# Value projections, a combination, gathers and the last block's running sums in other ticks of a hand-ordered megakernel

## The chip, the cores and the metric

One core of one Trainium2 chip runs one program. The metric is the device time of an execution in microseconds. TensorE (PE), VectorE (DVE), ScalarE (ACT), GpSimd (POOL) and the sync engine (SP, which only issues transfers) each run an instruction stream of their own and meet at semaphores.

## The reference, cut to what matters

x is 16 sequences of 256 tokens with 128 features, all fp32. Two layers, each `x = x + s * silu(g)` with s and g computed from the layer-normed x:

```
layer 0: s = causal softmax attention (16 heads of 64) @ Wo + bo
         g = shared FFN (352 wide) + the FFN of the token's best of 8 experts
layer 1: s = linear attention: phi = elu + 1, 16 heads of 8,
             num, den = running sums over the sequence of k*v and of k
         g = a network of 2 layers, each:
             h = shift_token(x); q, k, v = h @ wqkv   (8 heads of 64)
             q, k normed, rotated (xpos); attention in a window of 64 tokens
             x = x + o @ wo
             h = layer norm of shift_token(x); a, g = h @ w1 + b1
             x = x + (a * gelu(g)) @ w2 + b2
```

## The kernel before

The tokens are worked through in 8 blocks (b = 0 to 7) of 512 tokens: two sequences, four tiles of 128 tokens. All attention is done in steps of one form, whatever the layer: for a pair of heads and one sequence, TensorE computes logits, VectorE adds the mask and takes the maximum (L1041, "masked"), ScalarE takes exponentials (L871, L872, "exps"), TensorE transposes them (L595), VectorE and ScalarE copy the result out (L1052, L886), TensorE multiplies with the values (L615 or L629, "values"), and for every second step a transposition of the inverse sums (L639, "merge") is copied out by ScalarE (L849) and multiplied on (L1063).

The order is written out by hand in the class `Plan`. It makes a list of ticks; a tick holds at most one attention step, and `self.put(tick, name, ...)` lays side work into a tick. Every engine then walks through the same ticks and emits its share in a fixed order: TensorE emits the projections or transpositions of q and k for a later step ("produce"), the step's logits, the previous step's transpositions, the side work, and then the product of values two steps back and its merge. ScalarE emits its copies, then the side work, then the exponentials, then the merge's copy. VectorE emits masking, copy and scaling first and the side work last. GpSimd and SP do only side work, and GpSimd the expansion of the inverse sums (L1341). A tick is no barrier: each queue runs in order and as far ahead as its semaphores let it.

A block's softmax attention has the name (0, b, half, pair), and its first ticks are f0 (half 0) and f1 (half 1). The ticks from block 1 on repeat every 36. The side work that the change touches:

- `v` (b, half, t): value projection of tile t of a half, one product of 512 columns on TensorE (L545) and one copy on ScalarE (L849). Values are needed two ticks behind f0 or f1.
- `down0`, `comb` (b): the shared FFN's second product (L672) and, on VectorE, the addition of the expert's result (L1094); then the combination: a tanh on ScalarE (L915) and three operations on VectorE (L1100, L1102, L1104). Both stand at tick c of the block, `comb` one tick later where `late` is set (blocks 3 to 6).
- `r` (b): four indirect gathers of the expert results from DRAM, issued by GpSimd (L1377), into the buffer `c.r` that is also `c.xn0`. `held` is the planner's list of tick spans in which that buffer is in use; `down0` waits for the gathers.
- `kv`, `cum`, `sum`, `o1`, `oT`, `s1` (b): the linear attention. `kv` forms the products k*v of a tile on GpSimd (L1441, 1152 columns) and adds two tiles (L1445); `cum` is the running sum of one of eight chunks, one product on TensorE (L740), a copy on ScalarE (L900) and four operations on GpSimd (L1411 to L1416); `sum` reduces the chunk on VectorE (L1206); `o1` divides, `oT` transposes, `s1` is the output product (L751). In ticks they are laid out from l0 on.

The other side work named below: `qkv`, `mix`, `rot`, `rr`, `kn` make q and k of the windowed attention: a square and a copy on ScalarE (L950, L951), the rotary products on VectorE (L1227, L1231, L1236) and GpSimd (L1456, L1457), an inverse root by Newton steps on VectorE in twelve small instructions of 64 columns (L1241, L291 to L296), and the scaling of the keys (L1327). `ln2`, `ln2n`, `yT` are the second layer norm: moments and inverse root on VectorE, whitening (L315), transposition on TensorE (L540). `ffn` is the shared FFN's first product.

All products on TensorE are fp32 and take two passes, so one product is two records; transpositions take one.

## Time and profile before

| | us |
|---|---|
| median of 3 runs | 2084.16 (2081.3 to 2085.23) |
| the profiled execution | 2096.84 |
| its span | 2095.0 |
| mean granted clock of TensorE in it | 0.918 |
| busy: TensorE products / weight loads | 1780.8 / 1150.7 |
| busy: VectorE / ScalarE / GpSimd | 1283.2 / 1186.3 / 868.5 |

A busy figure is the time in which the engine executed something; idle time is noted at the instruction that ends it, with what released it. The granted clock is TensorE's, as a share of 2.4 GHz; it has the values 1 and 0.5, and a stretch shows the mean. Times inside the execution are counted from the start of its span. The chain of waits runs 48% on TensorE, 20% on VectorE and 7% on ScalarE. Transfers take part in the first 270 us mostly; after that the 16 DMA engines are nearly idle.

Which tick stands where in the trace was found by counting instructions in program order. Tick 80 starts on TensorE at about 578 us, tick 116 at 805, tick 152 at 1037, tick 188 at 1269, tick 224 at 1501, tick 256 at 1708, tick 286 at 1915 and tick 299 at 2013.

### The profile page before, as it was taken

To read this page: it belongs to the slowest core of one execution; us is meant where nothing else is said; L and a number is where in the kernel's file an instruction comes from. 1 tells how busy PE (TensorE), PEld (TensorE's weight loads), DVE (VectorE), ACT (ScalarE), POOL (GpSimd) and SP (SyncE) were. 2 spreads that over 40 slices of the span, in tenths; PEclk is the share of its full clock that TensorE was granted. 3 is DMA by queue.
4 is the path that set the end of the run, shared out by engine and by line. 5 is a ranking of instruction groups with operands and counts; after the bars stand their busy time and mean duration, and the time that the engine had idled before them with its cause. 6 is when DMAs were issued, how large, how long until landed. Compare 5 with 4: busy or idle time off the path is not lost.

```text
span 2095.0 us, 38065 instructions
## 1 busy us (share of the span) xinstructions
PE 1780.8 (85%) x12532; PEld 1150.7 (55%) x12532; DVE 1283.2 (61%) x4211; ACT 1186.3 (57%) x3527; POOL 868.5 (41%) x993
## 2 busy tenths in 40 slices
PE   6679988998989888998889988988889897785876
PEld 4358754654566455664565456554556455463554
DVE  4434446556675567566756566656756656868663
ACT  2444547565756575657656675657556565553643
POOL 2633215533535334432544344533553345646410
PEclk9889999999999999999999999999999998898978
DMA  8146600000000000000000000000000000000000
GB/s 230 52 157 208 193 16 1 11 1 1 6 2 16 1 1 6 6 12 1 6 1 17 1 1 6 16 1 1 6 2 11 0 6 1 1 7 0 1 1 11
DMA packets 49725, 53.48 MB, mean 26 GB/s; under 512 B 6387, under 2 KB 42237, under 8 KB 49533
## 3 DMA queue, kind: packets, MB, share of 16 engines
q0 software_dynamic: 7808, 27.79, 4.0%
q1 hardware_dynamic: 41724, 23.26, 3.9%
q8 instruction: 104, 1.70, 0.3%
q14 instruction: 89, 0.72, 0.1%
HBM read 41.60 MB, written 9.44 MB: 24 GB/s over the span
## 4 chain that ended last, share of the span: by engine, by line
PE 48%; DVE 20%; ACT 7%; issue 6%; POOL 1%; DVEq 0%; ACTq 0%; POOLq 0%
PE ps L595 5%; PE ps L657 4%; PE ps L554 3%; PE ps L732 3%; PE ps L574 3%; DVE p L1041 3%; DVE big L1231 3%; PE ps L615 3%; PE ps L629 2%; PE ps L639 2%; DVE ss L1227 2%; PE ps L564 2%; PE ps L783 2%; PE ps L774 2%; PE ps L776 2%
## 5 line engine op out<-in xcount | busy, mean ns | idle before, releaser
L1341 POOL COPY rdx<-rden 128x256 f32<-128x256 f32 x256 | 100.8, 423 | 659.0 <-DVE rden L1058 633.9
L1041 DVE CUSTOM_DVE_ANT_0 p<-ps,mask 128x128 f32<-128x128 f32 (+1 forms) x512 | 152.2, 353 | 222.7 <-PE ps L587 216.5
L1041 DVE CUSTOM_DVE_ANT_0 p<-ps,mask,nrq 128x128 f32<-128x128 f32 x512 | 148.8, 346 | 189.1 <-PE ps L583 188.3
L595 PE MATMUL ps<-ident,p 128*128 128x128 f32 x1280 | 223.8, 300 | 27.0 <-ACT p L872 25.2
L871 ACT ACTIVATE p<-p,nmax 128x128 f32<-128x128 f32 x512 | 200.2, 391 | 52.9 <-DVE nmax L1041 52.6
L872 ACT ACTIVATE p<-p,nmax 128x128 f32<-128x128 f32 (+1 forms) x512 | 226.2, 442 | 0.0
L886 ACT ACTIVATE pt<-ps 128x384 f32<-128x384 f32 (+1 forms) x256 | 111.7, 436 | 195.8 <-PE ps L595 194.3
L732 PE MATMUL ps<-wqkv,hT 128*128 128x512 f32 x384 | 197.2, 622 | 27.5 <-ACT big L951 25.8
L595 PEld LDWEIGHTS ps<-ident,p 128*128 128x128 f32 x1280 | 146.4, 149 | 106.6 <-issue 91.0
L574 PE MATMUL ps<-k,q 64*128 64x128 f32 x1024 | 132.1, 335 | 45.1 <-DVE nmax L1041 24.2
L574 PEld LDWEIGHTS ps<-k,q 64*128 64x128 f32 x1024 | 82.0, 194 | 148.6 <-issue 85.3
L1052 DVE COPY pt<-ps 128x384 f32<-128x384 f32 (+1 forms) x256 | 124.4, 486 | 59.0 <-PE ps L595 58.9
L564 PE MATMUL ps<-ident,big 128*128 128x128 f32 x512 | 86.5, 308 | 80.2 <-DVE big L1236 37.1
L1456 POOL TENSOR_TENSOR big<-big,rots 128x512 f32<-128x512 f32 x64 | 98.1, 1533 | 124.5 <-ACT big L951 124.5
L554 PE MATMUL ps<-xnT,w 128*128 128x512 f32 x256 | 148.3, 665 | 0.9 <-ACT v L849 0.9
L615 PEld LDWEIGHTS ps<-pt,v 128*64 128x64 f32 (+1 forms) x2048 | 107.2, 138 | 71.7 <-issue 49.7
L615 PE MATMUL ps<-pt,v 64*64 64x64 f32 (+2 forms) x2048 | 143.2, 258 | 0.2 <-PE ps L615 0.2
L732 PEld LDWEIGHTS ps<-wqkv,hT 128*128 128x128 f32 x384 | 62.9, 190 | 129.3 <-ACT big L951 77.9
L657 PE MATMUL ps<-wo,attT 128*128 128x128 f32 x1024 | 125.1, 282 | 7.5 <-DVE nmax L1041 5.1
L657 PEld LDWEIGHTS ps<-wo,attT 128*128 128x128 f32 x1024 | 120.9, 197 | 12.9 <-DVE nmax L1041 9.4
L849 ACT ACTIVATE rT<-ps 128x512 f32<-128x512 f32 x128 | 74.8, 584 | 82.0 <-PE ps L639 81.4
L564 PEld LDWEIGHTS ps<-ident,big 128*128 128x128 f32 x512 | 65.2, 158 | 96.8 <-issue 68.7
(255 smaller groups left out, 4151.0 us busy)
## 6 DMA issues: line engine op xcount, KB each, us to landing
slots_in<-xn SPq DMA_DIRECT2D x1, 2560.0 KB, 14.3
v<-slots_in SPq DMA_DIRECT2D x20, 128.0 KB
slots_out<-v SPq DMA_DIRECT2D x20, 128.0 KB
big<-in_x SPq DMA_DIRECT2D x4, 512.0 KB, 6.0
x<-in_x SPq DMA_DIRECT2D x8, 256.0 KB, 3.9
out_x<-x SPq DMA_DIRECT2D x8, 256.0 KB, 2.3
wqkv<-in_wqkv SPq DMA_DIRECT2D x2, 768.0 KB
xn<-in_x SPq DMA_DIRECT2D x6, 256.0 KB, 3.1
```

The costliest lines, as they stand in the source:

```text
L554: MM(bank[:, :], c.wqk[which][:, a:a + P], c.xnT[:, st.b % 2, :], start=True, stop=True).then_inc(c.mm_full, 1)
L564: last = nc.tensor.transpose(bank[:, t * P:(t + 1) * P], c.qkr[:, t, a:a + P], c.ident[:, :])
L574: MM(banks[h][:, 0:P], q[f:f + HD, 0:P], k[f:f + HD, 0:P], start=True, stop=True)
L595: last = nc.tensor.transpose(bank[:, j * P:(j + 1) * P], c.p[:, u % 4, j * P:(j + 1) * P], c.ident[:, :])
L615: last = MM(bank[f:f + HD, q + at:q + end], v[keys, 2 * st.s + t, a:a + HD], pts[h][keys, at:end], **flags)
L657: last = MM(bank[:, t * P:(t + 1) * P], c.attT[kind][:, i, t * P:(t + 1) * P], w, start=i == 0, stop=i == END)
L732: MM(bank[:, :], c.hT[:, t * P:(t + 1) * P], c.wqkv[:, l, i * INNER1:(i + 1) * INNER1], start=True, stop=True).then_inc(c.mm_full, 1)
L871: A(p[:, 0:P], p[:, 0:P], ACT.Exp, bias=c.nmax[:, u % 4, 0:1], scale=-1.0, accum_out=den[:, 0:1])
L872: A(p[:, P:end], p[:, P:end], ACT.Exp, bias=c.nmax[:, u % 4, 1:2], scale=-1.0, accum_out=den[:, 1:2])\
L886: A(c.pt[:, u % 4, 0:end], c.pt_ps[pt.slot("t", st.n, 1)][:, 0:end], ACT.Copy).then_inc(c.pt_done_act, 1)
L1041: last = V.tensor_tensor_reduce(out=c.p[:, u % 4, a:b], in0=bank[:, a:b], in1=mask, scale=scale, scalar=3e38, op0=ALU.add, op1=ALU.min, ac ...
L1052: V.tensor_copy(c.pt[:, u % 4, 0:end], bank[:, 0:end]).then_inc(c.pt_done, 1)
```

## The change

Nothing is computed otherwise and nothing is added or left out; instructions change their place in the queues. In ticks, as the planner's rules give them before and after:

| side work | blocks | before | after |
|---|---|---|---|
| `v` half 0, tile 2 | 3 to 7 | 71, 107, 143, 179, 215 | 70, 106, 142, 178, 214 |
| `v` half 1, tiles 0 and 1 | 3 to 7 | 80, 116, 152, 188, 224 | 87, 123, 159, 195, 231 |
| `v` half 1, tiles 2 and 3 | 3 to 7 | 88, 124, 160, 196, 232 | 97, 133, 169, 205, 241 |
| `r` | 3 to 6 | 114, 150, 186, 222 | 110, 146, 182, 218 |
| `comb` | 3 to 6 | 117, 153, 189, 225 | 116, 152, 188, 224 |
| `kv` tiles 0, 1 | 7 | 279, 280 | 289, 290 |
| `kv` tiles 2, 3 | 7 | 285 | 295 |
| `cum`, eight chunks | 7 | 281, 282, 285, 286, 289 to 292 | 291, 292, 295, 296, 299 to 302 |
| `sum`, eight chunks | 7 | a tick behind each | a tick behind each |
| `o1`, `oT`, `s1` | 7 | 295, 297, 298 | 305, 307, 308 |

All else keeps its tick, and the number of ticks stays 322. The span in which the buffer of the gathers counts as held grows from three ticks to seven for blocks 3 to 6.

```diff
--- before.py
+++ after.py
@@ -224,7 +224,7 @@
                 self.put(a + 3 + t, "lin", b, t)
                 self.put(a + 5 + t, "phi", b, t)
             self.qkv_stages(a + 4, b, 0)
-            l0 = self.first[(1, b, 0, 0)] + (7 if b == LAST else 0)
+            l0 = self.first[(1, b, 0, 0)] + (17 if b == LAST else 0)
             for t in range(2):
                 self.put(l0 - 1 + t, "kv", b, t)
             for n, at in enumerate((1, 2, 5, 6, 9, 10, 11, 12)):
@@ -251,26 +251,27 @@
                 assert x1 > shared[b - 2], b
             for t in range(TILES):
                 if b:
-                    self.put(f0 - (2 if b < XRING else 11 - t // 2), "v", b, 0, t)
-                self.put(f1 - 3 if b < XRING else f0 - 1 if t < 2 else f0 + 7, "v", b, 1, t)
+                    self.put(f0 - (2 if b < XRING else 11 - t // 3), "v", b, 0, t)
+                self.put(f1 - 3 if b < XRING else f0 + 6 if t < 2 else f1, "v", b, 1, t)
             late = 4 if XRING <= b < LAST else 0
             for half in range(2):
                 self.put(self.end[(0, b, half, PAIRS - 1)] + 4 + (late - 1 if late and half else 0), "wo", 0, b, half)
             c = max(self.end[(0, b, 1, PAIRS - 1)] + 4, e_end + 3) + late
-            while any(c - 3 - late <= y and x <= c + 1 for x, y in busy) or any(c - 2 <= y and x <= c for x, y in held):
+            ahead = 6 if late else 2
+            while any(c - 3 - late <= y and x <= c + 1 for x, y in busy) or any(c - ahead <= y and x <= c for x, y in held):
                 c += 1
             assert c < lead[b] - (8 if 0 < b < LAST else 0), (b, c, lead[b])
             for ch in range(3):
                 self.put(c - 3 - late + ch, "ffn", b, ch)
             if b >= XRING:
                 at = max(f1, self.end[(1, b - XRING, 1, PAIRS - 1)] + 12)
-                assert at <= c - 2, (b, at, c)
+                assert at <= c - ahead, (b, at, c)
                 self.put(at, "xres", b)
             shared[b] = c - 1
-            held.append((c - 2, c))
-            self.put(c - 2, "r", b)
+            held.append((c - ahead, c))
+            self.put(c - ahead, "r", b)
             self.put(c, "down0", b)
-            self.put(c + (late > 0), "comb", b)
+            self.put(c, "comb", b)
             busy.append((c - 3 - late, c + 1))
         self.length = max(len(self.ticks), max(self.side) + 1) + 4
```

## Rows read from the trace of the kernel before

**Rows 1.** Table of stretches: busy us (instructions) by engine, granted clock, DMA share.

```profile
821.00:1051.00 230.00, 203.61 (x1445) 127.58 (x1446) 149.86 (x498) 141.00 (x424) 98.27 (x112) 0.94 0.02 6
...
1888.00:2013.00 125.00, 83.57 (x557) 52.44 (x557) 93.74 (x194) 58.49 (x153) 64.61 (x62) 0.81 0.00 1
```

**Rows 2.** VectorE in time order (start, us, operation, idle before), ticks 116 to 120.

```profile
816.37 0.69 DVE L1094 TENSOR_TENSOR ff<-ps,xn 128x512 f32<-128x512 f32 x1 [0.97 <-PE ps L672]
...
820.97 0.29 DVE L1041 CUSTOM_DVE_ANT_0 p<-ps,mask 128x128 f32<-128x128 f32 x1 [3.91 <-PE ps L587]
...
824.00 2.60 DVE L1102 TENSOR_TENSOR ff<-ff,s_sb 128x512 f32<-128x512 f32 x1
...
836.84 0.35 DVE L1041 CUSTOM_DVE_ANT_0 p<-ps,mask,nrq 128x128 f32<-128x128 f32 x1 [2.71 <-PE ps L583]
```

**Rows 3.** VectorE in order of time, block 2's combination and the ticks behind.

```profile
560.47 0.69 DVE L1094 TENSOR_TENSOR ff<-ps,xn 128x512 f32<-128x512 f32 x1 [1.99 <-PE ps L672]
...
562.58 0.69 DVE L1102 TENSOR_TENSOR ff<-ff,s_sb 128x512 f32<-128x512 f32 x1
...
591.31 0.28 DVE L1041 CUSTOM_DVE_ANT_0 p<-ps,mask 128x128 f32<-128x128 f32 x1
...
604.75 0.35 DVE L1041 CUSTOM_DVE_ANT_0 p<-ps,mask,nrq 128x128 f32<-128x128 f32 x1 [1.14 <-PE ps L583]
```

**Rows 4.** TensorE in order of time, around ticks 116, 124 and 134.

```profile
816.17 1.02 PE L545 MATMUL ps<-w,xnT 128*128 128x512 f32 x2
...
858.35 0.63 PE L540 MATMUL ps<-ident,h 128*128 128x128 f32 x4 [2.99 <-DVE h L315]
...
859.94 3.24 PE L545 MATMUL ps<-w,xnT 128*128 128x512 f32 x4 [0.26 <-ACT xT L968]
...
918.18 1.08 PE L540 MATMUL ps<-ident,h 128*128 128x128 f32 x4 [2.82 <-DVE h L315]
```

**Rows 5.** All engines in order of time, 815 to 832 us: GpSimd's key-value product.

```profile
823.38 2.67 POOL L1441 TENSOR_TENSOR big<-qkb,v 128x1152 f32<-128x1152 f32 x1
```

**Rows 6.** VectorE in order of time, first masking of tick 125.

```profile
866.50 0.35 DVE L1041 CUSTOM_DVE_ANT_0 p<-ps,mask,nrq 128x128 f32<-128x128 f32 x1 [6.88 <-PE ps L583]
```

**Rows 7.** ScalarE in order of time, end of the exponentials of tick 123.

```profile
854.61 0.19 ACT L872 ACTIVATION_READ_ACCUMULATOR p<-p,nmax 128x1 f32 x1
```

**Rows 8.** Table of stretches, behind the layer norm's transposition of tick 134.

```profile
917.00:923.80 6.80, 5.62 (x21) 3.47 (x22) 4.19 (x19) 3.39 (x11) 0.00 (x0) 0.51 0.00 0
```

**Rows 9.** VectorE in order of time, scaling of the keys in tick 107.

```profile
748.53 2.84 DVE L1327 TENSOR_TENSOR big<-big,rr 128x512 f32<-128x512 f32 x4
```

**Rows 10.** The gathers' line (min/median/max ns), then GpSimd, then VectorE in order of time.

```profile
L1377 POOL DMA_INDIRECT xn<-slots_out,pos_i x32: 940/955/1891, 284.3 to 1702.4; - x32
...
771.45 0.74 POOL L1341 COPY rdx<-rden 128x256 f32<-128x256 f32 x2 [3.35 <-DVE rden L1058]
...
775.40 1.26 POOL L1457 TENSOR_TENSOR big<-big,rots 128x512 f32<-128x512 f32 x1
...
782.03 1.30 DVE L1236 TENSOR_TENSOR big<-big 128x1024 f32<-128x1024 f32 x1
```

**Rows 11.** Table of stretches, the small instructions of the last two rotary steps.

```profile
1921.70:1933.60 11.90, 0.54 (x3) 0.14 (x1) 11.50 (x12) 0.60 (x1) 11.09 (x9) 0.50 0.00 0
...
2001.10:2003.90 2.80, 2.75 (x14) 2.45 (x14) 2.42 (x12) 0.98 (x2) 0.00 (x0) 0.50 0.02 6
```

**Rows 12.** VectorE in order of time, ticks 286 and 287.

```profile
1925.35 2.14 DVE L295 TENSOR_TENSOR scratch<-scratch,ss 128x64 f32<-128x64 f32 x1
...
1935.05 1.23 DVE L1206 TENSOR_REDUCE v<-v 128x36 f32<-128x288 f32 x2
```

**Rows 13.** GpSimd in order of time, tick 285.

```profile
1923.02 4.38 POOL L1441 TENSOR_TENSOR w<-attT 128x1152 f32<-128x1152 f32 x2
...
1927.48 2.61 POOL L1445 TENSOR_TENSOR w<-w 128x1152 f32<-128x1152 f32 x1
```

**Rows 14.** TensorE in order of time, tick 298.

```profile
2009.58 1.92 PE L751 MATMUL ps<-lwo,xT 128*128 128x128 f32 x8
```

## Prediction, before the changed kernel was run

> **What bounds the kernel now.** I read the table of stretches first, then the chain of waits, then the order of time around each place that the change touches. In one period of 36 ticks (one block's softmax attention and one block's second branch, 230 us) TensorE is busy for 203.6 us, VectorE for 149.9, ScalarE for 141 [rows 1]. So TensorE sets the time, and what can be won in a period is its idle time and the stretches in which it runs at 1.2 instead of 2.4 GHz. In the last stage VectorE has 93.7 of 125 us and the granted clock is 0.81 [rows 1]: there VectorE's own chain (rotary products, norms, running sums) sets the time.  The dates below are those of block 3's combination and block 4's value projections, which repeat every 231 us.
>
> **Part 1: the combination of blocks 3 to 6 one tick earlier, two value projections out of that tick.** Tick 116 ends on VectorE with the addition at 816.37, over at 817.06. Then it idles 3.91 us until the logits of tick 117 come (820.97), because TensorE first does two value projections (1.88 us, at 816.17) [rows 2, 4]. In tick 117 the combination's second product took 2.60 us (824.00), and the next masking stands behind it [rows 2]. In block 2, whose combination already stands in the tick of the addition, the same product took 0.69 (562.58); with a third operation of the same length behind it the combination is over at 564.0, 3.5 us after the start of the addition (560.47) [rows 3]. So after the change: addition at 816.4, combination over at 819.9, masking of tick 117 at 819.9 instead of 821.0. From there the three following ticks without a combination took 604.75 - 591.31 = 13.4 us in block 2's place [rows 3], against 836.84 - 820.97 = 15.9 now [rows 2]. Together 1.1 + 2.5 = 3.6; I take 3.3 for small waits that I don't see, with 1.9 (the projections alone) and 4.1 as ends. Four times: **-13.2 us**.
>
> A mechanism stands behind the 2.60. GpSimd's product of 1152 columns starts at 823.38 and takes 2.67, to 826.05 [rows 5]; VectorE's product of 0.69 starts at 824.00 and ends at 826.60, about 0.55 after it [rows 2]. It did not run slowly, it waited GpSimd's instruction out. By the Trainium skill (SBUF — State Buffer, Who interferes with whom) the port pair that VectorE and GpSimd share is an exclusive lock, held for a whole instruction; the trace agrees with these two rows. The same rule speaks against this change in its last part, below.
>
> **Part 2: the pair of value projections at the two later places.** Today the second pair stands in tick 124 behind the transposition at 858.35, in the open: 3.24 us for four passes at 859.94, while VectorE idles 6.88 us before the masking at 866.50 [rows 4, 6]. Removed from there the pair gives 3.24 + 0.26 of wait = 3.5 if the low clock goes with it, and 1.9 + 0.2 if it stays; I take 2.8. Five blocks (3 to 7): **-14.0 us**.
> It is paid where it lands. The pairs go into the ticks of the layer norm's inverse root (123 and 133, and those of the other blocks), where TensorE idles 2.99 us before 858.35 and 2.82 before 918.18, waiting for VectorE's whitening [rows 4]. A pair at full clock is 1.88. On ScalarE its two copies stand in front of the exponentials of that tick, which now end at 854.80 (854.61 + 0.19) [rows 7]; they end some 1.3 us later, the next transpositions with them, about 1.4 us before the whitened rows come at 858.35. So the pair is hidden in the normal case; I take 0.3 for each of ten places (0 to 1.0): **+3.0 us**. If the cover is gone, a pair costs 1.9 at the high clock and 3.24 at the low one.
> After the idle time before 918.18 the transposition of four tiles took 1.08 us, against 0.63 at 858.35 [rows 4]: the granted clock is 0.51, the 1.2 GHz level, from 917.0 to 923.8, with TensorE busy for 5.62 us of it [rows 8]. With the pair in it the idle time falls from 2.82 to about 1.1 us, and the drop may go away. Its whole price there is half of the 5.62, 2.8 us; I take half, five times: **-7.0 us** (0 to -14).
>
> **Part 3: one of the four first-half projections from tick 107 to 106.** Less is won than it seems: the keys that TensorE transposes next wait for VectorE's four products from 748.53 to 751.37 [rows 9], so the product of tick 107 may be early but the next tick isn't. 0.2 each: **-1.0 us** (0 to -1 each).
>
> **Part 4: the gathers four ticks earlier.** The issue of one gather holds GpSimd for 0.94 to 1.89 us (32 of them), so a block's four hold it for 3.8 to 7.6 [rows 10]. The addition that waits for their data starts at 816.37 when TensorE is done [rows 2], so it doesn't wait for them today and nothing is won. In tick 110 they stand in front of the copy at 771.45, the bias additions of tile 1 and the rotary product of tile 0, whose last half ends at 776.66. GpSimd idles 3.35 us there, so the three come 0.5 to 4.2 us later; VectorE uses the rotary product at 782.03, 5.4 us after its end [rows 10]. So **0**, between -0.5 and +1.5, four times. SP's queue is not passed; the loads keep their ticks.
>
> **Part 5: the last block's running sums ten ticks back.** In the last stage twelve small VectorE instructions took 11.9 us (1921.7 to 1933.6) while GpSimd was busy for 11.1; the same twelve took 2.8 in 2001.1 to 2003.9 with GpSimd idle [rows 11]. One of them, of 64 columns, took 2.14 [rows 12]. Now GpSimd does the last block's key-value products there (4.38 for two, 2.61 for their sum [rows 13]). What follows when they are put ten ticks back:
> - First collision. Its two reductions of 1.23 us a pair [rows 12] that stood before the keys' scaling leave: -2.5. The lock goes only in part. The products of tiles 0 and 1, planned for tick 289, wait for nothing late, so GpSimd runs ahead to them as soon as it is through tick 285, and these 7.0 us come over VectorE's last two rotary steps and a part of the same twelve instructions. Of the 9.1 us I take 4.8. Together -7.3.
> - Two chunks fewer in ticks 289 and 290: -2.0. The output product of 1.92 us at 2009.58 [rows 14], which stands between the keys and the next logits, leaves: -1.9.
> - Second collision. The products of tiles 2 and 3 land in tick 295, in front of the same twelve instructions of the last block, which are free today: 7.0 for the two products and their sum, 1.2 for the reductions that now stand before the keys' scaling: +8.2.
> - The rest goes into the attention of ticks 299 to 308. Four reductions of 1.23 are partly in VectorE's idle time; the chunks' copies stand in front of the exponentials on ScalarE; and the output product (1.92) stands on TensorE in front of the last product of values. 6.5, between 2 and 11.
> Sum: -7.3 - 2.0 - 1.9 + 8.2 + 6.5 = **+3.5 us**, between -6 and +16. By the lock of the skill the twelve wait for whole GpSimd instructions, as counted; if GpSimd's work did not slow them, the second collision would cost 1.2 and the first would give 2.5 + 9.1, and the last stage would come out near -8.
>
> **Sum:** -13.2 - 14.0 + 3.0 - 7.0 - 1.0 + 0 + 3.5 = -28.7 us of the profiled execution's 2096.8, which lies 12.7 above the median of the runs. Scaled to the median (x 0.994): 2084.2 - 28.5 = **2055.6 us**.
>
> **Rivals.**
> (a) The end costs more: both collisions stay whole, and all of ticks 299 to 308 is in the open, +16 instead of +3.5: 2068. For it speaks that GpSimd runs ahead; against, that the first collision has less work to wait for.
> (b) Masking of tick 118 is held by something other than the combination (the copies between query and key on ScalarE), and part 1 gives nothing: 2084.2 - 15.4 = 2069. Block 2's place, which looks like the planned one, speaks against it. This is also the case that moving one tick does not do what it says.
> (c) The moved pairs are in the open at their new places at the high clock: ten times 1.9 instead of 0.3, and no clock won: -28.7 + 16 + 7 = -5.7, 2078.5.
> (d) All covers hold and the low clock goes everywhere: -16.4 - 17.5 - 14 - 1 - 4 = -53: 2031.
> (e) Slower. The moved pair runs at the low clock, ahead of the whitening: 3.24 us on TensorE and its copies in front of the exponentials, at ten places. The margin is about 1.4 us; if the pair is in the open whole, ten times 3.24 stand against 13.2 + 5 x 2.1 + 1.0 = 24.7: with the end's 3.5 it is +11, 2095. It decides from 2.1 us in the open at each place. Against it: the pair itself keeps TensorE at work there, and its idle time of today begins only behind it.
>
> **How the numbers follow.** My forecast has 0.52 (2046 to 2064), (a) 0.14, (b) 0.10, (c) 0.08, (d) 0.10, (e) 0.06. The range 2040 to 2074 takes in (a) and (b) and leaves out most of (c), (d) and (e). About 0.2% (4.2 us) is what a measurement of this kernel can tell from no change. Faster 0.90, within 0.2% 0.05 (half of (c) and a little of (a)), slower 0.05.
>
> **What would show it.** Part 1: the combination's middle product at 0.69 us in the profile after, and 13 to 14 us from the masking of tick 117 to that of tick 120. Part 2: idle before the layer norm's transposition down from 2.99 and 2.82 to about 1 us, the row of 3.24 us gone, VectorE's 6.88 down to 3 or 4. Clock: fewer low stretches, a mean above 0.93 in a period. A period of 225 us instead of 231. Part 5: two stretches with small instructions of over 0.6 us instead of one. I would be wrong most likely by the size of the end, or if the idle time before the transposition stays while VectorE's chain itself comes later.

## The result, and the profile after

The changed kernel takes **2064.31 us** (median of 4 runs, 2061.97 to 2064.36) against 2084.65 (median of 4, 2081.3 to 2085.23): ratio 0.990, interval 0.9888 to 0.9913, 20.3 us faster. The forecast was 2055.6, between 2040 and 2074: the sign was right and the time lies inside the range; 8.7 us of the gain did not come, and one of the parts had the wrong sign.

| | before | after |
|---|---|---|
| median, us | 2084.65 | 2064.31 |
| the profiled execution, us | 2096.84 | 2064.33 |
| its span, us | 2095.0 | 2062.5 |
| mean granted clock | 0.918 | 0.933 |
| busy: TensorE / VectorE / GpSimd, us | 1780.8 / 1283.2 / 868.5 | 1760.4 / 1278.5 / 863.4 |

The profiled execution of before lies 12 us above its median and that of after at its median, so the 32.5 us between the two profiles overstate the gain. The mean clocks give the time at 1.2 GHz: 2 x (1 - 0.918) x 2095 = 344 us before, 2 x (1 - 0.933) x 2062.5 = 276 after. If all of it lay over work in the open, half of the difference, 34 us, would be won; where it lies over idle time or over hidden work nothing is, so this is an upper bound. TensorE's own busy time, with the same instructions, fell by 20.4 us.

The page after: the busy line, the granted clock in 40 slices, and the engines' shares of the chain that ended last.

```profile
PE 1760.4 (85%) x12532; PEld 1140.4 (55%) x12532; DVE 1278.5 (62%) x4211; ACT 1186.3 (58%) x3527; POOL 863.4 (42%) x993
...
PEclk9889999999999999999999999999999998897968
...
PE 47%; DVE 20%; ACT 7%; issue 6%; POOL 1%; DVEq 0%; ACTq 0%; POOLq 0%
```

The table of stretches of after answers to [rows 1]: one period (from the addition of block 3 to that of block 4) and the last stage. Its columns are us, then the busy us of TensorE, its weight loads, VectorE, ScalarE and GpSimd, the granted clock, the DMA share and GB/s.

```profile
811.20:1036.50 225.30, 203.78 (x1462) 127.90 (x1462) 147.78 (x498) 142.86 (x430) 95.97 (x112) 0.95 0.02 6
1851.00:1976.70 125.70, 80.93 (x540) 51.16 (x540) 90.12 (x179) 56.42 (x148) 62.74 (x49) 0.80 0.00 1
```

A period takes 225.3 us. Before, from addition to addition, it took 231.9 (816.37 to 1048.29). The last stage is as long as it was (125.7 us for 125).

**Ticks 116 to 120.** VectorE after, in order of time (start, us; idle time before it in brackets). It answers to [rows 2].

```profile
811.17 0.69 DVE L1095 TENSOR_TENSOR ff<-ps,xn 128x512 f32<-128x512 f32 x1 [1.59 <-PE ps L673]
...
813.28 0.69 DVE L1103 TENSOR_TENSOR ff<-ff,s_sb 128x512 f32<-128x512 f32 x1
...
814.62 0.28 DVE L1042 CUSTOM_DVE_ANT_0 p<-ps,mask 128x128 f32<-128x128 f32 x1
...
826.08 0.35 DVE L1042 CUSTOM_DVE_ANT_0 p<-ps,mask,nrq 128x128 f32<-128x128 f32 x1 [1.14 <-PE ps L584]
```

The combination's middle product is down from 2.60 to 0.69, and from the addition to the masking of tick 120 it is 14.9 us instead of 20.5.

**Ticks 124 and 134.** The layer norm's transpositions on TensorE, then the first masking of tick 125 on VectorE and the stretches behind the transpositions. They answer to [rows 4, 6, 8].

```profile
847.61 0.94 PE L541 MATMUL ps<-ident,h 128*128 128x128 f32 x4 [1.74 <-DVE h L316]
...
906.78 0.63 PE L541 MATMUL ps<-ident,h 128*128 128x128 f32 x4 [1.57 <-DVE h L316]
...
855.09 0.35 DVE L1042 CUSTOM_DVE_ANT_0 p<-ps,mask,nrq 128x128 f32<-128x128 f32 x1 [6.21 <-PE ps L584]
...
847.00:855.00 8.00, 7.39 (x45) 4.50 (x45) 1.88 (x11) 3.92 (x12) 4.83 (x5) 0.57 0.01 3
905.40:912.20 6.80, 5.29 (x28) 3.10 (x29) 5.57 (x23) 4.63 (x14) 1.45 (x3) 1.00 0.00 0
```

Both idle times shrank (2.99 to 1.74, 2.82 to 1.57). At 906.78 the low clock is gone; at 847.61 it is there, over work that is in the open, so that the masking of tick 125 comes 7.5 us behind the transposition, where it was 8.2 before with 3.24 us of projections in between. These two are not alike at all five blocks. From the layer norm's transposition to the next tick's masking it was 8.1 to 8.5 us before, and is 5.9, 7.5, 5.9, 5.9 and 7.4 now, where the next 8 us are at 0.79, 0.57, 0.79, 0.79 and 0.57. Behind the transpositions of tick 134 and its sisters the next 6.8 us are at 0.75, 1.00, 0.75, 0.75 and 1.00.

### The profile page after: what moved, and what is told of

It is laid out like the page before. It is cut to its first block, busy times and chain, and to the rows that moved or that the text cites. A ratio compares the mean times of both kernels' runs of the same rounds, so it can differ in the third digit from the quotient of the medians.

```text
span 2062.5 us, 38065 instructions
## 1 busy us (share of the span) xinstructions
PE 1760.4 (85%) x12532; PEld 1140.4 (55%) x12532; DVE 1278.5 (62%) x4211; ACT 1186.3 (58%) x3527; POOL 863.4 (42%) x993
## 4 chain that ended last, share of the span: by engine, by line
PE 47%; DVE 20%; ACT 7%; issue 6%; POOL 1%; DVEq 0%; ACTq 0%; POOLq 0%
PE ps L596 5%; PE ps L658 5%; PE ps L733 3%; PE ps L616 3%; PE ps L575 3%; PE ps L555 3%; DVE p L1042 3%; DVE big L1232 3%; PE ps L640 2%; PE ps L565 2%; DVE ss L1228 2%; PE ps L784 2%; PE ps L630 2%; PE ps L775 2%; PE ps L777 2%
## 5 line engine op out<-in xcount | busy, mean ns | idle before, releaser
L575 PE MATMUL ps<-k,q 64*128 64x128 f32 x1024 | 133.2, 338 | 37.8 <-DVE nmax L1042 17.2
L850 ACT ACTIVATE k<-ps 128x512 f32<-128x512 f32 x128 | 74.9, 585 | 81.6 <-PE ps L565 42.1
```

The source lines that it names most:

```text
L575: MM(banks[h][:, 0:P], q[f:f + HD, 0:P], k[f:f + HD, 0:P], start=True, stop=True)
L850: A(dst, mm_bank(*name)[:, :], ACT.Copy).then_inc(c.mm_done, 1)
```

## Experiments

Intervals are those of the ratio to the kernel before; the runs of a table's block shared one chip.

| | kernel | ratio | interval | profiled span, clock |
|---|---|---|---|---|
| parts alone | combination | 0.9936 | 0.9923 to 0.9949 | 2085.4, 0.921 |
| | half-1 pairs | 0.9904 | 0.989 to 0.9918 | 2076.9, 0.926 |
| | half-0 projection | 1.0066 | 1.0047 to 1.0085 | 2111.8, 0.921 |
| | last block | 1.0007 | 0.9992 to 1.0021 | 2096.0, 0.921 |
| from the changed one | half-0 back | 0.9839 | 0.982 to 0.9858 | 2046.5, 0.933 |
| | added products, 107 | 0.9827 | 0.9809 to 0.9845 | 2058.7, 0.936 |
| | pair to 115 | 0.985 | 0.9827 to 0.9872 | 2053.3, 0.931 |
| | split pair | 0.9797 | 0.9777 to 0.9818 | 2051.0, 0.935 |
| from the changed one | itself | 0.9896 | 0.987 to 0.9921 | 2067.4, 0.928 |
| | later products | 0.9895 | 0.987 to 0.992 | 2064.7, 0.930 |
| | gathers back | 0.9881 | 0.9854 to 0.9907 | 2065.8, 0.927 |
| from the changed one, by itself | split pair, added products, 116 | 0.9796 | 0.9769 to 0.9822 | 2044.8, 0.940 |

The kernels "pair to 115", "split pair" and the last one have the half-0 projection back as well.

In microseconds of a time of 2096.5 (the median of before in the first block) the four parts alone are -13.4, -20.1, +13.8 and +1.5. Their sum is -18.2, the whole change -20.3: the parts add up within their intervals, and one of them costs what another one gives. The gathers (part 4 of the prediction) were not tried alone in the kernel before; they were taken back in the changed one.

### The combination alone

```
-            self.put(c + (late > 0), "comb", b)
+            self.put(c, "comb", b)
```

> The kernel before with one part of the change: the combination of blocks 3 to 6 stands in the tick of the addition; the value projections stay where they were. Theory (from the two traces): the gain of part 1 is the combination's, not the projections', and it is bigger than in my sum, because TensorE's idle time of about 3 us in front of tick 119 goes and the low clock behind it goes too. 4.0 to 4.5 us at each of four places: 16 to 18 us faster. Rival (the sum on record): 2.5 us at each place without any gain of clock, 10 us faster. Second rival (b of the prediction): masking of tick 118 is held by something else, within 2 us of the kernel before. In the profile: the product of the combination at 0.69 us and no stretch of 1.2 GHz in tick 119.

Measured: -13.4 us (-10.7 to -16.1), between the theory (16 to 18, at its lower end) and the rival (10, outside). VectorE's maskings of ticks 118 and 120 and the table of stretches over all of it:

```profile
826.58 0.29 DVE L1041 CUSTOM_DVE_ANT_0 p<-ps,mask 128x128 f32<-128x128 f32 x1 [1.27 <-PE ps L587]
...
835.12 0.35 DVE L1041 CUSTOM_DVE_ANT_0 p<-ps,mask,nrq 128x128 f32<-128x128 f32 x1 [1.13 <-PE ps L583]
...
818.00:836.00 18.00, 17.08 (x170) 12.20 (x169) 9.82 (x42) 14.28 (x48) 5.44 (x6) 1.00 0.00 1
```

The addition stands at 818.51 here, so it is 16.6 us to the masking of tick 120, against 20.5: 3.9 us won. The clock is 1.00 throughout, where the kernel before shows this in tick 119:

```profile
831.00:836.00 5.00, 5.00 (x40) 3.59 (x40) 2.31 (x11) 3.04 (x11) 2.36 (x3) 0.66 0.02 3
```

5.0 us of work with 0.34 of clock missing are 1.7 us: this is what my sum had left out. Of the 3.9 us some 0.5 are given back further on: from addition to addition it is 228.5 us here (818.51 to 1047.00) against 231.9, 3.4 less, and four times 3.4 is what the runs show.

### The half-1 pairs alone

```
-                self.put(f1 - 3 if b < XRING else f0 - 1 if t < 2 else f0 + 7, "v", b, 1, t)
+                self.put(f1 - 3 if b < XRING else f0 + 6 if t < 2 else f1, "v", b, 1, t)
```

> The kernel before with the two pairs of half-1 value projections moved (116 to 123, 124 to 133, and so on), nothing else. Theory (from the two traces): what leaves tick 124 in the open comes back for the most part, because the low clock stays in tick 124 and now lies on other work; 0.6 to 2.6 us at each of five places, and 1.0 to 2.2 at each of the five places of tick 133, and next to nothing from tick 116 without the combination's move: together 14 to 18 us faster. Rival (the sum on record): 14.0 + 7.0 - 3.0 + 4 times 1.1 = 22 us faster.

Measured: -20.1 us (-17.2 to -23.1): it takes in the sum on record (22) and just touches my correction of it (14 to 18). Behind the transposition of tick 134 the stretch is

```profile
906.50:911.00 4.50, 4.39 (x19) 2.74 (x20) 3.11 (x15) 3.13 (x10) 0.00 (x0) 0.62 0.00 0
```

Half of the low clock of tick 134 is left, where the changed kernel has none at this place with the same instructions there. That of tick 119 stays (0.66 from 821.0 to 826.0), as it must if it is the combination's.

### The half-0 projection alone

```
-                    self.put(f0 - (2 if b < XRING else 11 - t // 2), "v", b, 0, t)
+                    self.put(f0 - (2 if b < XRING else 11 - t // 3), "v", b, 0, t)
```

> The kernel before with one projection of half 0 moved from tick 107 to 106 (and at four other places). Theory (from the two traces): 1.5 us lost at each of five places, 7 us slower: tick 107 becomes shorter, the keys of tick 108 come no earlier, so TensorE idles about 2 us in front of tick 108 and runs its first work there at 1.2 GHz, work that ran at 2.4 GHz in the kernel before. Rival (the sum on record): 1 us faster, not to be told from no change.

Measured: **+13.8 us** (+9.9 to +17.8): the sign of the theory and twice its size. First the transposition of the keys of tick 108 and the stretch behind it in the kernel before, then the same in the changed kernel, then with this part alone.

```profile
751.52 1.06 PE L564 MATMUL ps<-ident,big 128*128 128x128 f32 x8
...
751.50:755.50 4.00, 4.00 (x37) 3.02 (x36) 1.67 (x9) 3.83 (x15) 0.00 (x0) 1.00 0.01 2
```

```profile
744.42 1.06 PE L565 MATMUL ps<-ident,big 128*128 128x128 f32 x8 [2.01 <-DVE big L1328]
...
744.40:749.80 5.40, 5.38 (x34) 3.89 (x35) 1.67 (x9) 2.31 (x7) 0.00 (x0) 0.68 0.01 2
```

```profile
752.64 1.94 PE L564 MATMUL ps<-ident,big 128*128 128x128 f32 x8 [3.65 <-DVE big L1327]
...
750.90:758.30 7.40, 5.66 (x30) 4.22 (x30) 3.27 (x12) 1.82 (x4) 0.45 (x1) 0.54 0.00 1
```

The keys come from VectorE at the same time as ever: in all three kernels their transposition starts 7.6 us behind the first transposition of tick 107. That one is, in the kernel before and with this part alone,

```profile
743.93 1.09 PE L564 MATMUL ps<-ident,big 128*128 128x128 f32 x4 [3.62 <-DVE big L1236]
```

```profile
745.04 0.63 PE L564 MATMUL ps<-ident,big 128*128 128x128 f32 x4 [2.60 <-DVE big L1236]
```

So in the kernel before the low clock fell on tick 107, which had time to spare in front of the keys, and tick 108 began without idle time at 2.4 GHz. The moved projection changes two idle times. In tick 106 it shortens the one in front of tick 107 (3.62 to 2.60 us), and the transposition there runs at the full clock. In tick 107 it is missing, TensorE stands 2.0 to 3.7 us in front of the keys, and the low clock falls on tick 108, all of which is in the open. From the transposition of the keys to tick 109's second one it is 5.5 us before (751.52 to 757.05), 6.9 in the changed kernel (744.42 to 751.35) and 7.8 with the part alone (752.64 to 760.45): 1.4 and 2.3 us lost. The same stretch of 5.4 us is at 0.68 at all five places of the changed kernel, and at 1.00 at all five of the kernel before.

The time at 1.2 GHz as a whole hardly changes. By the medians of the runs on this chip (mean clock 0.920 of 2110 us, 0.922 of 2095) it is 338 us against 327, which costs 5.4 us at most. The rest of the 13.8 is a matter of which work the low clock covers, and the mean clock does not show that.

The five places of the keys account for some 10 of the 13.8 us. A part of the rest is further on: from the addition of tick 116 to the masking of tick 120 it takes 21.3 us here (820.29 to 841.61) and 20.5 before. Why a shift by 1 us lengthens a low stretch 80 us later I can't say from the rows.

### The last block's sums alone

```
-            l0 = self.first[(1, b, 0, 0)] + (7 if b == LAST else 0)
+            l0 = self.first[(1, b, 0, 0)] + (17 if b == LAST else 0)
```

> The kernel before with the last block's running sums ten ticks further back, nothing else. Theory (the sum on record, which the two traces bear out so far): relief of 9 to 10 us before tick 296, a collision with GpSimd's two products in tick 296 of 8 us, and 6 us in the attention of ticks 299 to 308: 3 to 4 us slower. Rival: GpSimd's work doesn't hold VectorE's small instructions, 8 us faster. Second rival: everything in the open, 16 us slower.

Measured: +1.5 us (-1.7 to +4.4), which agrees with the sum on record (+3.5) and excludes both rivals. TensorE's transpositions of the keys after the two collisions, in the kernel before and then with this part alone:

```profile
1938.83 1.94 PE L564 MATMUL ps<-ident,big 128*128 128x128 f32 x8 [16.59 <-DVE big L1327]
...
2007.85 1.94 PE L564 MATMUL ps<-ident,big 128*128 128x128 f32 x8 [2.25 <-DVE big L1327]
```

```profile
1931.18 1.94 PE L564 MATMUL ps<-ident,big 128*128 128x128 f32 x8 [10.25 <-DVE big L1327]
...
2007.82 1.94 PE L564 MATMUL ps<-ident,big 128*128 128x128 f32 x8 [10.63 <-DVE big L1327]
```

7.7 us are won by the first (0.5 of them in front of the last stage) and all of them are gone by the second.

### The changed kernel with the half-0 projection back

```
-                    self.put(f0 - (2 if b < XRING else 11 - t // 3), "v", b, 0, t)
+                    self.put(f0 - (2 if b < XRING else 11 - t // 2), "v", b, 0, t)
```

> The changed kernel with one part undone: the half-0 projection of tile 2 back from tick 106 to 107 (and at the four other places). Theory (the low clock lies on work that was hidden behind the wait for the keys when the projection stands in tick 107, and on work in the open when it stands in 106): tick 108 runs at 2.4 GHz again, 1.5 us at each of five places, 7 us faster than the changed kernel, ratio to the kernel before near 0.987 where the changed kernel has 0.990. Rival (the part is worth what the sum on record says): 1 us slower than the changed kernel, ratio 0.9905. Second rival: the 13.8 us that this part cost alone all come back, ratio 0.9835.

Measured: ratio 0.9839, against 0.9896 of the changed kernel (measured on another chip, each beside the kernel before): 12 us faster, give or take 7. That is the second rival's number, and the theory's 7 is not excluded. The transposition of the keys and the stretch behind it:

```profile
745.15 1.06 PE L565 MATMUL ps<-ident,big 128*128 128x128 f32 x8 [0.20 <-DVE big L1328]
...
745.10:750.50 5.40, 4.55 (x38) 3.36 (x38) 1.67 (x9) 4.97 (x19) 0.00 (x0) 1.00 0.01 2
```

The idle time of 2.01 us is 0.20, and tick 109's second transposition on TensorE starts 5.5 us behind this one (750.68) instead of 6.9 (751.35). The mean clock is 0.933, as in the first profile of the changed kernel. Five times 1.4 is 7 us; more comes in ticks 116, 152, 188 and 224, where the addition's products take 3.87, 3.45, 4.16 and 3.60 us instead of 4.67, 4.61, 4.63 and 4.93. That is a low clock that got shorter at a place which the edit does not touch.

### The changed kernel with more work in tick 107

```
+        if b >= XRING and half == 0 and t == 3:
+            MM(bank[:, :], c.xnT[:, b % 2, t * P:(t + 1) * P], c.wv[:, half * 512:(half + 1) * 512],
+               start=True, stop=True)
         MM(bank[:, :], c.xnT[:, b % 2, t * P:(t + 1) * P], c.wv[:, half * 512:(half + 1) * 512],
            start=True, stop=True).then_inc(c.mm_full, 1)
```

> The changed kernel with more work: in tick 107 the projection of tile 3 is done twice on TensorE (the first product's result is overwritten; five products of two passes more). No instruction is moved. If the cost of part 3 is the clock behind TensorE's idle time in front of tick 108, the added 1.0 us lies in that idle time, the time is no longer and, where the low stretch of tick 108 goes, 1.5 us shorter at each of five places: between 0 and 7 us faster than the changed kernel. Rival (the copies on ScalarE or the order of the values' product are the cause): the added products are in the open or change nothing, 0 to 5 us slower.

Measured: ratio 0.9827, as good as the projection moved back, with nothing moved and 5 products added. TensorE, the two projections of tile 3 in tick 107 (the first is the added one) and the transposition of the keys, and the stretch behind that:

```profile
743.85 1.91 PE L547 MATMUL ps<-w,xnT 128*128 128x512 f32 x2
745.56 1.06 PE L549 MATMUL ps<-w,xnT 128*128 128x512 f32 x2
...
748.57 1.06 PE L568 MATMUL ps<-ident,big 128*128 128x128 f32 x8 [1.15 <-DVE big L1331]
...
748.50:753.00 4.50, 4.43 (x38) 3.37 (x38) 1.67 (x9) 3.25 (x13) 0.00 (x0) 1.00 0.01 2
```

The idle time is 1.15 us instead of 2.01. The copies on ScalarE and the order of the rest are those of the changed kernel, so the gain can't come from them, and TensorE's clock is what is left: the mean clocks of the runs are 0.934 to 0.940, those of the changed kernel 0.927 to 0.934. Where it acts is shown in part. In the profiled execution (the slowest of its five runs) the stretch behind the keys is at full clock at two of the five places and at 0.68 at the other three, and the addition's products take 3.52 and 3.62 us in two of their four ticks and 4.93 and 4.86 in the others. By the ratios 14 us are gained, more than these places give.

### The first half-1 pair in tick 115

```
-                self.put(f1 - 3 if b < XRING else f0 + 6 if t < 2 else f1, "v", b, 1, t)
+                self.put(f1 - 3 if b < XRING else f0 - 2 if t < 2 else f1, "v", b, 1, t)
```

with the half-0 projection back.

> The changed kernel with the half-0 projection back in tick 107 and the first half-1 pair (of blocks 3 to 7) in tick 115 instead of 123, behind the output product, in front of TensorE's idle time of 3.95 us. Theory: the pair (2.05 us) is hidden there, and filling half of the idle time takes the stretch of 1.2 GHz from tick 116, in which the addition's products run 4.67 us: 1.6 to 2.7 us at four places, 6 to 11 us faster than the kernel with the half-0 projection back, less what tick 124 loses when its idle time grows to about 3 us again (0 to 2 us each). Rival: the low clock stays in tick 116 in spite of the pair, or the pair's copies hold the exponentials: no faster, up to 5 us slower than the kernel with the half-0 projection back.

Measured: ratio 0.985, not to be told from 0.9839. The logits of tick 116 and the addition's products:

```profile
803.48 0.49 PE L575 MATMUL ps<-k,q 64*128 64x128 f32 x4 [2.24 <-DVE s_sb L1073]
...
805.10 4.25 PE L673 MATMUL ps<-sh,ff 128*128 128x128 f32 x24
```

The pair is hidden and the logits are at full clock (0.49; 0.80 in the kernel without this move), but the products of the addition take no less: 4.25, 3.64, 4.86 and 4.20 us at the four places, where the kernel with only the half-0 projection back has 3.87, 3.45, 4.16 and 3.60. The idle time that the pair had filled in front of tick 124 is 2.99 again, and the 8 us behind it are at 0.60. One hole was filled by opening another.

### The first pair split around the logits of tick 124

```
+                if b >= XRING and t == 1:
+                    self.side[f0 + 7].insert(0, ("v", b, 1, t))
+                else:
```

with the half-0 projection back.

> The changed kernel with the half-0 projection back in tick 107 and, of the pair of tick 123, the second projection in tick 124 in front of the layer norm's transposition, in whose idle time of 1.74 us it lies. Theory: the idle time falls to about 0.8 us, the stretch of 1.2 GHz from 847.5 to 855 (6.8 us, half of it lost time) goes: 3 us at each of five places, 15 us faster than the kernel with the half-0 projection back. Rival: what sets the clock is the time before as well (TensorE was idle twice in a row there), the low stretch stays, and nothing is won (within 3 us).

Measured: ratio **0.9797**, 8.8 us (of 2090; give or take 6) better than without the split; the theory had said 15. TensorE in tick 160, and the stretch behind the transposition; below them that stretch at the same place in the kernel without the split.

```profile
1069.58 1.02 PE L549 MATMUL ps<-w,xnT 128*128 128x512 f32 x2
...
1072.32 0.63 PE L544 MATMUL ps<-ident,h 128*128 128x128 f32 x4 [1.72 <-DVE h L319]
...
1072.30:1080.30 8.00, 7.98 (x56) 4.57 (x57) 3.46 (x20) 6.02 (x16) 6.03 (x6) 1.00 0.00 1
```

```profile
1068.40:1076.40 8.00, 7.94 (x56) 4.54 (x57) 3.50 (x20) 5.98 (x16) 5.99 (x6) 1.00 0.00 1
```

Tick 160 alone shows nothing: its clock was up without the split too. Over the five places (ticks 88, 124, 160, 196, 232) the 8 us behind the transposition are at 1.00, 0.57, 1.00, 1.00 and 1.00 with the split and at 0.57, 0.61, 1.00, 0.60 and 1.00 without it, so it went up at two. My reason was wrong: the idle time did not shrink (1.72), since the projection only changed sides with the logits and VectorE's chain is what ends it. That the low stretch goes because the idle time shrinks is refuted; why it goes stays open.

### The changed kernel itself

> The changed kernel itself once more, beside the kernel before on this chip and beside the next two kernels: ratio 0.990, within 0.988 and 0.992. In the profile the stretches of 1.2 GHz behind the layer norm's transposition of tick 124 and its four sisters differ from those of the first profile if their coming is not settled by the order of the instructions; they are the same if it is.

Measured: 0.9896, and the stretches differ. This is tick 160 in the first profile of the changed kernel, and then in the second one of the same program:

```profile
1072.90:1080.90 8.00, 7.94 (x52) 4.98 (x53) 3.35 (x20) 4.84 (x14) 5.32 (x6) 0.79 0.00 1
```

```profile
1078.29 0.80 PE L541 MATMUL ps<-ident,h 128*128 128x128 f32 x4 [1.72 <-DVE h L316]
...
1078.20:1086.20 8.00, 7.91 (x49) 5.02 (x50) 1.80 (x12) 3.92 (x12) 5.49 (x6) 0.57 0.00 1
```

The same instructions behind the same idle time run at 0.57 for 8 us here and at 0.79 in the first profile. It is not a matter of two chips only: the next kernel below ran on the same chip as this profile and differs from it in nothing before the last stage, and it shows 0.79 at this place (from 1075.3). Over the span it is 2 x 0.072 x 2067.4 = 298 us at 1.2 GHz against 276, for 4.9 us more. So a difference of one place between two profiles does not show what an edit does there; ratios of runs do.

### The last key-value products behind the scaling

```
-                        self.put(l0 + at, "kv", b, t)
+                        self.put(l0 + at + (2 if b == LAST else 0), "kv", b, t)
```

> The changed kernel with the last block's second pair of key-value products (and their sum) in tick 297 instead of 295, behind the expansion that needs VectorE's inverse of that tick, so that they can't run over the last rotary step's twelve small instructions. Theory (these instructions wait for GpSimd's): the twelve take 2.8 us instead of 7.1 and what stands in front of them 3 us less, 7 us; the products come over the scaling of the keys instead, which costs 1 to 5: together 2 to 6 us faster than the changed kernel. Rival (the 8 us lost in tick 296 have another cause): the twelve instructions still take 7 us and the time is the same or longer.

Measured: no difference (0.9895 against 0.9896). In the changed kernel: the last rotary operation, the second of the twelve small instructions, the stretch of all twelve and the scaling of the keys, then GpSimd's products and their sum:

```profile
1954.76 3.12 DVE L1237 TENSOR_TENSOR big<-big 128x1024 f32<-128x1024 f32 x1
...
1960.05 2.65 DVE L292 TENSOR_SCALAR scratch<-ss 128x64 int32<-128x64 int32 x1
...
1957.80:1967.20 9.40, 3.60 (x24) 2.87 (x24) 9.01 (x13) 0.98 (x2) 7.60 (x6) 0.50 0.00 0
...
1969.45 2.68 DVE L1328 TENSOR_TENSOR big<-big,rr 128x512 f32<-128x512 f32 x4
...
1953.60 6.36 POOL L1442 TENSOR_TENSOR w<-attT 128x1152 f32<-128x1152 f32 x2
...
1960.04 2.61 POOL L1446 TENSOR_TENSOR w<-w 128x1152 f32<-128x1152 f32 x1
```

and the rotary operation, the stretch and the scaling with the products two ticks later:

```profile
1956.88 1.70 DVE L1237 TENSOR_TENSOR big<-big 128x1024 f32<-128x1024 f32 x1
...
1958.50:1963.00 4.50, 3.60 (x24) 2.87 (x24) 4.12 (x13) 0.98 (x2) 2.06 (x3) 0.50 0.00 0
...
1965.28 9.12 DVE L1328 TENSOR_TENSOR big<-big,rr 128x512 f32<-128x512 f32 x4
```

The twelve and the operation in front of them are 4.9 + 1.4 = 6.3 us faster, and the scaling of the keys is 6.4 slower (four instructions; 9.12 for 2.68), because the products run over it now. The collision moved with the products: that GpSimd's instructions hold VectorE's is shown at both ends. The small instruction of 2.65 us ends at 1962.70, GpSimd's sum at 1962.65. I had put the new collision at 1 to 5. By the Trainium skill (SBUF — State Buffer, the section "SBUF: two separate sides") a GpSimd instruction and a VectorE instruction that needs the shared port pair (with two inputs in SBUF, against a GpSimd instruction that reads SBUF, or in a two-port mode) exclude each other, and whichever starts first has the pair for its whole instruction. These rows agree, and they show it in both directions (two of GpSimd's products took 6.36 us in the changed kernel, 4.38 in [rows 13]). The scaling has two inputs; the small instruction has one, and whether it ran in a two-port mode no row shows.

### The gathers back

```
-            ahead = 6 if late else 2
+            ahead = 2
```

> The changed kernel with the gathers of blocks 3 to 6 back in the tick two before the addition (114 instead of 110), nothing else. Sum on record: part 4 is worth 0, between -0.5 and +1.5 us for a block, so the same time within 2 us. Rival (the gathers' data hold the addition or its products now that the combination stands in the addition's tick): up to 1.4 us lost at each of four places, 2 to 6 us slower than the changed kernel.

Measured: ratio 0.9881 against 0.9896: 3 us in favour of the gathers where they were, give or take 8, so no difference that can be told. Of the rival (2 to 6 us slower when moved back) only the upper end is excluded. The addition waits for TensorE as before (1.23 us, at 818.25).

### The split pair, with added products in tick 116

The half-0 projection is back here too.

```
+            for _ in range(again):
+                MM(bank[:, :], c.wqk[which][:, a:a + P], c.xnT[:, st.b % 2, :], start=True, stop=True)
             MM(bank[:, :], c.wqk[which][:, a:a + P], c.xnT[:, st.b % 2, :], start=True, stop=True).then_inc(c.mm_full, 1)
...
-            produce(which, st)
+            produce(which, st, 2 if tick in plan.refill else 0)
```

> The changed kernel with the half-0 projection back in tick 107 and the first half-1 pair split between tick 123 and the front of tick 124 (ratio to the kernel before 0.980), and with more work: in tick 116 and its three sisters the projection of q in front of TensorE's idle time of 3.6 to 4.0 us is done three times instead of once (eight products of two passes more, their results overwritten). Theory: 2.05 us of added work lie in that idle time and cost nothing; the stretch of 1.2 GHz behind it shrinks or goes, in which the logits take 1.42 and the addition's products 4.0 to 4.7 us, and 1.1 to 2.7 us are won at each of four places: ratio 0.975 to 0.978. Rival: a second idle time or the work before it keeps the low clock there, or the path at this place runs through VectorE's scaling of the keys: ratio 0.980 again. Slower than 0.982 would mean that the copy of q behind the added products holds the exponentials.

Measured: ratio 0.9796 (0.9769 to 0.9822), the rival's number, with the upper end of the theory (0.975 to 0.978) not excluded. In tick 116 the theory holds: the projection done three times, the logits behind 2.24 us of idle time, the addition's products, and the stretch:

```profile
801.82 1.98 PE L562 MATMUL ps<-xnT,w 128*128 128x512 f32 x4
...
806.90 0.49 PE L583 MATMUL ps<-k,q 64*128 64x128 f32 x4 [2.24 <-DVE s_sb L1081]
...
808.52 2.94 PE L681 MATMUL ps<-sh,ff 128*128 128x128 f32 x24 [0.15 <-DVE nmax L1050]
...
804.50:812.00 7.50, 5.11 (x57) 4.35 (x56) 6.00 (x21) 0.98 (x2) 0.00 (x0) 1.00 0.01 3
```

The products take 2.94 us instead of the 4.69 of the split pair's kernel. But this holds at two of the four places: in the four ticks they take 2.94, 4.50, 2.94 and 4.46 us here, and 4.69, 4.00, 4.35 and 4.21 with the split pair alone, so little is left over all four. The profiled span is 6.2 us shorter than the split pair's; the medians' ratios don't show it. It stays open whether the gain is real and small or a matter of that one execution. This kernel and the split pair's are the fastest here (2046.8 and 2049.1 us), some 21 us faster than the changed kernel by the ratios (0.98 against 0.99 of 2090).

## Why the prediction was right, and where it was wrong

**Part 1** (-13.2 for the combination and the projections of that tick together): the place, the lock and the 0.69 us came as said. The window was too small: 5.6 us from the addition to the masking of tick 120 instead of 3.3, above the upper end of 4.1. I had taken the ticks from the masking of 117 to that of 120 from block 2, where they take 13.4, and they took 11.5. TensorE's idle time of 3.06 us in front of tick 119's transposition went down to 0.78 with the combination, and the low clock behind it, 1.7 us of it, went too; I had not counted the clock.

**Part 2** (-14.0 + 3.0 - 7.0, with the pair's share of part 1 some -21): -20.1 alone. The cover held, and rivals (c) and (e) fell: the two copies and the pair delay nothing, the transpositions at 847.61 and 906.78 still wait 1.74 and 1.57 us for VectorE (I had said about 1.1). The -14.0 was too much: from the transposition to the next masking 2.2, 0.7, 2.5, 2.2 and 1.0 us were won, 8.7 together, because the low clock stayed and lies on other work after the projections have gone, which I had not thought of. So VectorE's wait of 6.88 us became 6.21 and not 3 or 4. The -7.0 was right: from the transposition of tick 134 and its sisters to a masking 22 us later 1.1 to 2.2 us were won, 7.8 together, with the low clock gone at two places and shorter at three. The rest of the sum's 21 was tick 117, 1.1 us at four places.

**Part 3** (-1.0, 0 to -1 each): **this is the step that failed.** Alone it cost 13.8 us, and undone it gave 12 (give or take 7). I had seen that the next tick waits for the keys, and priced the freed time at nothing. But the time that TensorE now stands idle sat in front of tick 108, and the low clock, which had fallen on a tick with time to spare, fell on one with none. I had drawn just this connection at tick 134, the other way round, and not asked it here. Without this part the change would have come out near 2051 (0.9839 of 2084.65), and the sum less its own part 3 was 2056.6.

**Part 4** (0): nothing speaks against it, and it is settled only within 8 us.

**Part 5** (+3.5 from -7.3 - 2.0 - 1.9 + 8.2 + 6.5): +1.5 alone. The first term measures 7.7 at the keys. From there to the keys behind the second collision the sum has -2.0 + 8.2 = 6.2, and it is 76.6 us for 69.0, 7.6 more, so that nothing of the gain is left (2007.82 for 2007.85; by the sum 1.1 should have been). The output product and the attention, -1.9 + 6.5 = 4.6 in the sum, came as 1.0. The terms of the lock were right within 2 us, and rival (a) fell.

**The sum.** The parts alone gave -13.4 - 20.1 + 13.8 + 1.5 = -18.2 against -28.7. The miss of 10.5 us is 14.8 of part 3 and 1.1 of the pairs, less 3.4 that the combination gave beyond its 10 and 2.0 that the end spared. So the combination and the end paid for a third of what part 3 had wrong: that the time came out 8.7 us from the forecast is partly luck. The largest term is the clock's as far as the added products show it, and so is the combination's extra by the rows of tick 119; in the sum the one had been left out at a cost and the other at a gain.

The mean clock of a period was to be over 0.93 and is 0.95, but it was 0.94 before, so this sign could not tell anything; over the whole span it went from 0.918 to 0.933. The period was to be 225 us and is 225.3, and the two slow stretches of small instructions are there (7.7 us at 1885.3 and 9.4 at 1957.8 for 2.8 in [rows 11]):

```profile
1885.30:1893.00 7.70, 1.09 (x4) 0.72 (x4) 7.29 (x15) 0.60 (x1) 4.76 (x2) 0.50 0.00 0
```

## What to carry to other kernels

When side work is taken out of a tick of the busiest engine, look at what that engine does with the freed time: if it stands idle in front of work on the critical path, that work can start at 1.2 GHz, and a projection of 1 us that is "hidden anyway" can be what holds the clock up, as it was here. Price every moved instruction at both of its places with the granted clock of the stretch behind each, and test it by putting work in, not only by taking it out. Compare each variant with the kernel that it was made from, and at every place that the edit touches: one place can differ between two profiles of the same program. An engine pair that locks is relieved by moving work only where the new neighbours are not on the path either.

## What the runs showed of the hardware that was not expected

- More work made the kernel faster: five products (two passes each; the one at 743.85 took 1.91 us) added in front of idle time took the ratio from 0.9896 to 0.9827.
- The clock behind the same idle time is not settled by the program: 0.79 and 0.57 over 8 us behind 1.7 us of idle time in tick 160 of two executions of the changed kernel. The Trainium skill (TensorE: Matmul & The Clock Gate, "What's actually happening") says that the number of slow products at a kernel's start varies from run to run. The two profiles show the like in the middle of a kernel.
- An idle time of 1.72 us was followed by the low clock (0.57, at 849.70) and by the full one (1.00, at 1072.32) in one execution of the kernel with the split pair, so the length of the last idle time alone doesn't say which it will be.
- A kernel can get slower with nearly the same mean clock: 0.920 with the half-0 projection moved alone and 0.922 in the kernel before (medians of the runs on one chip), at a ratio of 1.0066.
